# Attention's hand-written queues in a new order, in a three-stage decoder layer

## The chip, the core and the metric

The kernel runs on one core of one Trainium2 chip. The metric is the device time of one launch, in microseconds (us). Five engines work side by side, each through its own queue in program order, and meet only at semaphores: TensorE (PE; its weight loads are listed as PEld), VectorE (DVE), ScalarE (ACT), GpSimd (POOL), and SyncE (SP), which here only issues DMAs. An engine whose next instruction waits on a semaphore does nothing else meanwhile, so the order in which a queue is written decides what can run beside what.

## The reference, cut to what matters

The layer has three stages: a gated delta-rule attention, a state-space block, and a mixture-of-experts feed-forward. Only the attention is touched. For each of 16 heads and 4 batches of 512 tokens it computes:

```
q, k, v  = silu(causal conv of width 4 (x @ wq, wk, wv))          # 128 channels a head
gates    = small MLP of (entropy, |v - k@proxy|/|v|, cos, log1p|..|)   # 5 numbers a token
for rate in (slow, fast):                                          # two recurrences
    S_t  = S_{t-1} * decay_t + beta_t * k_t (v_t - k_t^T (S_{t-1} * decay_t))^T
    o_t  = q_t^T S_t
o        = lam * o_fast + (1 - lam) * o_slow
out      = o / rms(o) * onorm * sigmoid(gate)                      # then @ wo
```

## The kernel before, in words

Everything is float32, and a float32 matmul appears in the trace as two passes, so that every matmul of the program gives two weight loads and two MATMUL records.

**Units.** Head and batch make 64 units. A unit's 512 tokens are four chunks of 128, and there are two rates, so eight pairs of rate and chunk. `over_units` walks the slots: slots -3 to 5 are written out, then a loop of 13 turns (`TURNS`) runs four slots each, then the rest is written out. In slot `s` each engine's `slot(s)` works on several units at once, each at another stage of its life: `s.has(3)` and `s.has(2)` are units whose q, k and v are being projected, `s.has(1)` the unit whose gates and decay rows are made, `s.has(0)` the unit whose chunk matrices are built and inverted, `s.has(-1)` the one whose recurrence runs, `s.has(-2)` and `s.has(-3)` those whose output is normed and gated. `late` is the slot before. So each engine has one list of some 30 to 50 steps, which repeats once a unit, and `late` only says where the list is cut. The order in these lists is written by hand or by a planner outside; nothing in the kernel computes it.

**Steps on PE.** `project(i, k)` is one of four 128x512 matmuls that make k, v or q of a unit (L503). `products(level)` multiplies decayed keys with decayed keys and queries, in 32-wide blocks for levels 0 to 4 (L525: 32 small matmuls, 64 passes; I call these, and the next two, *fine groups*), wider ones for level 5 (L531) and 6 (L535). `w_fine_sum` (L549) and `x_fine_sum` (L560), levels 1 to 4, are the two halves of one step of a block inversion, again 64 passes each; `w_32_sum`, `xy_32_sum`, `w_64_sum` and `y_64_sum` (L627 to L658) are its wide end. `recur_even`, `recur_u`, `recur_odd` with a chunk number 0 to 3 are the recurrence over chunks (L573 to L616). `turn_v`, `proxy_v`, `gram_kq`, `turn_feats`, `hidden_1`, `hidden_2`, `heads_out`, `turn_rows` (L697) belong to the gates, `mean_square` (L692) and `gate_logits` (L706) to the output.

**The chain of levels.** `decay_nq(level)` on DVE (L1175 twice, then L1183) scales queries and keys for the next level: it waits for `products(level)` and `products(level + 1)` waits for it. `keep(level)` (L1194) masks a product into `apt_fine`, `grow(level)` (L1203, L1207) extends the inverse, `seed_y` and `turn_x0` start it. `copy_w` on ACT moves what `w_fine_sum` gave to SBUF for `x_fine_sum`.

**The chain of rows.** `heads_out` on PE, `add_z` on DVE, `tanh_t` on ACT, `gates_vals` on POOL, `turn_rows` on PE, `copy_rows` on ACT (L936); then SP (L447 to L456) writes the rows to DRAM, reads back the amplitude rows, then the amplitude sums, then the key rows, then the query rows, each hold waiting for the transfer before. `exp_e1` and `exp_tot` on ACT exponentiate them, `prepare_nq(NEG_K)` and `prepare_nq(QUERY)` on DVE (L1306, L1310) multiply them in, and `products(0)` of that unit waits for the last of these.

Of the kernel before, what the change touches and what calls it, by code (L numbers as in the profile page):

```python
# [136 lines left out]
def attn_stage(nc, io):  # L137

    with ExitStack() as ctx:
# [284 lines left out]
        with nc.Block() as block:  # L424
# [64 lines left out]
            def _(pe):  # L489
# [239 lines left out]
                def slot(s):  # L729
                    late = s.at(-1)  # L730
                    if late.has(0):
                        w_fine_sum(late, 2)
                    if late.has(-1):
                        recur_odd(late, 1)
                    if late.has(0):
                        products(late, 4)
                    if late.has(0):
                        x_fine_sum(late, 2)
# [4 lines left out]
                    if late.has(2):  # L743
                        gram_kq(late)
                    if late.has(0):
                        w_fine_sum(late, 3)
                    if late.has(0):
                        products(late, 5)
                    if late.has(-1):
                        recur_u(late, 2)  # L750
                    if late.has(-2):
                        mean_square(late)
                    if late.has(0):
                        x_fine_sum(late, 3)
                    if late.has(3):
                        project(late, 3, P_K, 2)
                    if late.has(3):
                        project(late, 3, P_K, 3)
                    if late.has(0):
                        w_fine_sum(late, 4)  # L760
                    if late.has(3):
                        project(late, 3, P_V, 0)
                    if late.has(-1):
                        recur_odd(late, 2)
                    if late.has(0):
                        x_fine_sum(late, 4)
# [4 lines left out]
                    if late.has(0):  # L771
                        w_32_sum(late)
                    if late.has(2):
                        turn_feats(late)
                    if late.has(-1):
                        recur_even(late, 3)
                    if late.has(3):
                        project(late, 3, P_V, 2)
                    if late.has(0):
                        xy_32_sum(late)  # L780
# [4 lines left out]
                    if late.has(-1):  # L785
                        recur_u(late, 3)
                    if late.has(0):
                        w_64_sum(late)
                    if late.has(-1):
                        recur_odd(late, 3)  # L790
                    if s.has(2):
                        project(s, 2, P_Q, 1)
                    if s.has(1):
                        hidden_1(s)
                    if s.has(2):
                        project(s, 2, P_Q, 2)
                    if late.has(0):
                        y_64_sum(late)
                    if s.has(0):
                        products(s, 0)  # L800
                    if s.has(-1):
                        recur_even(s, 0)
                    if s.has(2):
                        project(s, 2, P_Q, 3)
                    if s.has(-1):
                        recur_u(s, 0)
                    if s.has(1):
                        hidden_2(s)
                    if s.has(0):
                        products(s, 1)  # L810
                    if s.has(-1):
                        recur_odd(s, 0)
                    if s.has(1):
                        heads_out(s)
                    if s.has(2):
                        turn_v(s)
                    if s.has(0):
                        products(s, 2)
                    if s.has(-1):
                        recur_even(s, 1)  # L820
                    if s.has(0):
                        w_fine_sum(s, 1)
                    if s.has(2):
                        proxy_v(s)
                    if s.has(-3):
                        gate_logits(s)
                    if s.has(0):
                        x_fine_sum(s, 1)
                    if s.has(0):
                        products(s, 3)  # L830
                    if s.has(-1):
                        recur_u(s, 1)
                    if s.has(3):
                        project(s, 3, P_K, 0)
                    if s.has(1):
                        turn_rows(s)
# [4 lines left out]
            def _(act):  # L841
# [178 lines left out]
                def exp_tot(s):  # L1020
                    act.wait_ge(sums_in, s.due(1, 16, 16))
# [18 lines left out]
                def slot(s):  # L1040
                    late = s.at(-1)
                    if late.has(-1):
                        copy_kt(late, 0)
                    if late.has(-1):
                        copy_u(late, 0)
                    if late.has(1):
                        hide_2(late)
                    if late.has(2):
                        silu(late, 2, P_V)
                    if late.has(2):  # L1050
                        tap(late, 2, P_Q)
                    if late.has(-1):
                        copy_o(late, 0)
                    if late.has(1):
                        tanh_t(late)
                    if late.has(2):
                        keep_v(late)
                    if late.has(-2):
                        square_o(late)
                    if late.has(2):  # L1060
                        silu(late, 2, P_Q)
                    if late.has(0):
                        copy_w(late, 1)
                    if late.has(2):
                        square_v(late)
                    if late.has(-3):
                        tanh_gate(late)
                    if late.has(-1):
                        copy_kt(late, 1)
                    if late.has(-1):  # L1070
                        copy_u(late, 1)
                    if late.has(1):
                        copy_rows(late)
                    if late.has(-1):
                        copy_o(late, 1)
                    if late.has(0):
                        copy_w(late, 2)
                    if late.has(2):
                        square_vh(late)
                    if late.has(-1):  # L1080
                        copy_kt(late, 2)
                    if late.has(2):
                        square_err(late)
                    if late.has(0):
                        copy_w(late, 3)
                    if late.has(-1):
                        copy_u(late, 2)
                    if late.has(-2):
                        log_mean(late)
                    if late.has(3):  # L1090
                        tap(late, 3, P_K)
                    if late.has(0):
                        copy_32(late)
                    if late.has(2):
                        log_err(late)
                    if late.has(0):
                        copy_w(late, 4)
                    if late.has(-1):
                        copy_o(late, 2)
                    if late.has(1):  # L1100
                        exp_e1(late)
                    if late.has(1):
                        copy_ks(late)
                    if late.has(0):
                        copy_w(late, 5)
                    if late.has(0):
                        copy_64(late)
                    if late.has(2):
                        copy_feats(late)
                    if late.has(0):  # L1110
                        copy_xy32(late)
                    if late.has(3):
                        tap(late, 3, P_V)
                    if late.has(-1):
                        copy_u(late, 3)
# [4 lines left out]
                    if late.has(0):  # L1120
                        copy_w(late, 6)
                    if late.has(1):
                        exp_tot(late)
                    if s.has(1):
                        hide_1(s)
                    if late.has(-1):
                        copy_o(late, 3)
                    if late.has(3):
# [1365 lines left out]
```

## Time and profile before

| | us |
|---|---|
| median of 3 runs (lowest, highest) | 4910.75 (4907.41, 4925.25) |
| the profiled execution, and its span | 4893.68, 4891.9 |
| PE busy over the span | 4244.3 (87%) |
| DVE, ACT, POOL busy | 3329.3, 2248.5, 834.9 |

The attention fills the span from its start to about 3300 us; from 3400 us on the two other stages run. A busy PE is one with a matmul in flight. The idle time ahead of an instruction is put down to whatever released it; "issue" means that no semaphore explains it.

### The profile page before, as it was taken

The numbers are of one execution on the slowest core, as the hardware profiler recorded it, in microseconds if no ns is written. First come the engines' busy times: TensorE is split into PE (matmuls) and PEld (weight loads), VectorE is DVE, ScalarE is ACT, GpSimd is POOL, SyncE is SP. The second block draws the span as 40 slices with busy tenths as digits, with TensorE's granted clock in tenths as the row PEclk, the third lists the DMA queues.
The fourth block names the chain that finished last, engine by engine and source line by source line (L and its number), as shares of the span: only waits on it lengthen the run. The fifth ranks groups of instructions, "written<-read, shape, count | busy, mean of one in ns | idle before, by whom it ended". The sixth has DMA issues, their size and how long they took to land. (4 is left out here: it accounts for less than half of the span.)

```text
span 4891.9 us, 184831 instructions
## 1 busy us (share of the span) xinstructions
PE 4244.3 (87%) x76786; PEld 2657.1 (54%) x76786; DVE 3329.3 (68%) x5635; ACT 2248.5 (46%) x5484; POOL 834.9 (17%) x1800
## 2 busy tenths in 40 slices
PE   6789898988989888898988899975887786999999
PEld 4566666665666656666666666662333333444444
DVE  2678787777778777787777777864999995122121
ACT  2455565655556555555555555644344432111111
POOL 0222222322222222222222232220000000000000
PEclk9899999999999999999999999987898997999999
DMA  1111211112121111211111111112232334000000
GB/s 50 61 52 57 62 49 54 62 45 68 43 65 52 52 60 43 66 52 53 58 53 59 58 53 56 62 45 104 78 95 82 91 95 160 1 26 9 18 18 9
DMA packets 131630, 278.08 MB, mean 57 GB/s; under 512 B 20668, under 2 KB 62032, under 8 KB 127200
## 3 DMA queue, kind: packets, MB, share of 16 engines
q1 hardware_dynamic: 126176, 258.29, 16.8%
q8 instruction: 641, 10.50, 0.9%
q10 hardware_dynamic: 4608, 7.60, 0.4%
q14 instruction: 205, 1.68, 0.1%
HBM read 235.17 MB, written 30.67 MB: 54 GB/s over the span
## 5 line engine op out<-in xcount | busy, mean ns | idle before, releaser
L503 PE MATMUL a_pb<-a_x_t,a_w_qkv 128*128 128x512 f32 x1536 | 825.0, 634 | 24.4 <-DMA a_w_qkv<-in_w_qkv 12.2
L1175 DVE TENSOR_TENSOR a_nq<-a_nq,a_tot 128x512 f32<-128x512 f32 x768 | 516.8, 714 | 157.4 <-PE a_pb L535 62.1
L1151 DVE SCALAR_TENSOR_TENSOR a_acc<-a_pb,a_taps,a_acc 128x511 f32<-128x511 f32 (+2 forms) x576 | 429.7, 746 | 67.0 <-ACT a_acc L846 35.3
L1773 PE MATMUL m_p_y<-m_h,m_ident 128*128 128x512 f32 x512 | 292.2, 686 | 143.3 <-DVE m_h L1973 143.3
L525 PE MATMUL a_pb<-a_nq,a_ks 128*32 128x32 f32 x20480 | 250.6, 201 | 145.1 <-DVE a_ks L1183 126.6
L503 PEld LDWEIGHTS a_pb<-a_x_t,a_w_qkv 128*128 128x128 f32 x1536 | 250.4, 195 | 131.2 <-issue 104.6
L525 PEld LDWEIGHTS a_pb<-a_nq,a_ks 128*32 128x32 f32 x20480 | 218.6, 112 | 188.4 <-DVE a_nq L1175 135.2
L2241 PE MATMUL f_pb<-f_x_t,f_w_gu 128*128 128x512 f32 x704 | 308.0, 592 | 0.0
L549 PE MATMUL a_pb<-a_x_fine,a_apt_fine 32*32 32x16 f32 x16384 | 203.7, 183 | 107.3 <-issue 106.0
L1967 DVE TENSOR_TENSOR_SCAN m_h<-m_da,m_h 128x2048 f32<-128x2048 f32 x64 | 283.1, 4424 | 5.9
L549 PEld LDWEIGHTS a_pb<-a_x_fine,a_apt_fine 32*32 32x32 f32 x16384 | 173.5, 108 | 203.5 <-issue 189.8
L560 PEld LDWEIGHTS a_pb<-a_w_fine,a_y_fine 32*32 32x32 f32 x16384 | 176.9, 109 | 189.5 <-issue 178.9
L1183 DVE TENSOR_TENSOR a_ks<-a_ks,a_tot 128x512 f32<-128x512 f32 x384 | 274.5, 715 | 0.0
L2295 ACT ACTIVATE f_gate<-f_pb 128x512 f32<-128x512 f32 x132 | 78.8, 597 | 411.7 <-PE f_pb L2241 275.4
L1773 PEld LDWEIGHTS m_p_y<-m_h,m_ident 128*128 128x128 f32 x512 | 107.5, 220 | 293.4 <-DVE m_h L1973 170.2
L560 PE MATMUL a_pb<-a_w_fine,a_y_fine 32*32 32x16 f32 x16384 | 207.7, 183 | 66.1 <-issue 61.4
L1737 PE MATMUL m_p_o<-m_w_o,m_o_t 128*128 128x512 f32 x512 | 256.9, 622 | 0.0
L1194 DVE COPY_PREDICATED a_apt_fine<-a_mask_u,a_pb 128x256 f32<-128x256 int32 x320 | 179.4, 561 | 106.5 <-PE a_pb L549 106.4
L1896 ACT ACTIVATE m_da<-m_delta,m_neg_a 128x511 f32<-128x511 f32 x256 | 166.7, 711 | 182.5 <-DVE m_h L1967 180.1
L885 ACT COPY a_u_sb<-a_pb 128x256 f32<-128x256 f32 x256 | 95.4, 373 | 296.0 <-PE a_pb L593 296.0
L2241 PEld LDWEIGHTS f_pb<-f_x_t,f_w_gu 128*128 128x128 f32 x704 | 133.4, 190 | 166.4 <-issue 166.4
L2373 DVE TENSOR_TENSOR f_h_base<-f_gate,f_pb 128x512 f32<-128x512 f32 x44 | 30.2, 686 | 277.6 <-ACT f_gate L2295 277.6
(278 smaller groups left out, 8927.3 us busy)
## 6 DMA issues: line engine op xcount, KB each, us to landing
a_rows<-rows SPq DMA_DIRECT2D x192, 512.0 KB, 3.9
a_amp_sums<-amp_sums SPq DMA_DIRECT2D x64, 508.0 KB, 3.6
attn_o<-a_o_t SPq DMA_DIRECT2D x64, 256.0 KB, 2.6
m_b_rows<-ssm_bc SPq DMA_DIRECT2D x64, 256.0 KB, 3.7
m_c_rows<-ssm_bc SPq DMA_DIRECT2D x64, 256.0 KB, 4.6
m_o_t<-attn_o SPq DMA_DIRECT2D x14, 1024.0 KB, 8.6
a_w_qkv<-in_w_qkv SPq DMA_DIRECT2D x51, 256.0 KB, 2.8
f_w_gu<-in_w_gu SPq DMA_DIRECT2D x3, 1536.0 KB, 17.3
```

The lines of the kernel that those rows point to most:

```text
L503: mm = nc.tensor.matmul(pb[:, V_BANK if i == P_V else KQ_BANK], w_qkv[:, i, k], x_t[:, k, b * T:(b + 1) * T], start=(k == 0), stop=(k == D ...
L525: mm = nc.tensor.matmul(out.rearrange("p k (s h) -> p k s h", h=hs), ks[:, n2, rate, at], right(nq[:, n2, rate, :, at], hs), start=True, s ...
L549: mm = nc.tensor.matmul(w_psum[q, i].rearrange("p (s h) -> p s h", h=hs), apt_fine[q, i, NEG_K], left(x_fine[q, i:i + 1], hs)[:, 0], start ...
L560: mm = nc.tensor.matmul(x_psum[q, i], y_fine[q, i], w_fine[q, i], start=True, stop=True, tile_position=(g * BW, g * BW))
L1151: last = nc.vector.scalar_tensor_tensor(acc[:, i, d:T], src[:, 0:T - d], taps[:, i, 3 - d:4 - d], acc[:, i, d:T], ALU.mult, ALU.add)
L1175: last = nc.vector.tensor_tensor(part, part, spread(blocks, shape), ALU.mult)
L1183: nc.vector.tensor_tensor(part, part, spread(blocks.rearrange("p (s two) -> p s two", two=2)[:, :, 1:2], [P, T // hs, hs]), ALU.mult).then ...
L1194: nc.vector.copy_predicated(right(apt_fine[:].rearrange("p i k t -> p (i k) t"), hs), spread(compact(mask_u[:, level:level + 1], hs), [P, ...
L1737: mm = nc.tensor.matmul(p_o[:], o_t[:, q % 2, head], w_o[:, head], start=(head == 0), stop=(head == H - 1), skip_group_check=True)
L1773: nc.tensor.matmul(p_y[:, et], ident[:], h[:, (b * DS + n) % 3, et], start=(n == 0), stop=(n == DS - 1), skip_group_check=True).then_inc(s ...
L1967: nc.vector.tensor_tensor_scan(steps, da[:, row % 2].rearrange("p e t -> p (e t)"), steps, 0.0, ALU.mult, ALU.add).then_inc(scanned, 1)
L2241: mm = nc.tensor.matmul(out, w_gu[:, side, k, cols], x2_t[:, b % 2, k], start=(k == 0), stop=(k == DC - 1), skip_group_check=True)
```

## The change

The four lists are written in a new order; no matmul, vector or activation step is added or removed. Along with it come the edits that the new order needs:

```diff
 # PE: slot(), the list read round from its new start
+ x_fine 1, proxy_v, gate_logits, products 3, recur_u 1, turn_rows,
+ w_fine 2, recur_odd 1, mean_square, products 4, K 0, recur_even 2, K 1,
+ x_fine 2, recur_u 2, products 5, recur_odd 2, w_fine 3, gram_kq, K 2, recur_even 3, K 3,
+ x_fine 3, V 0, recur_u 3, w_fine 4, products 6, V 1, x_fine 4, V 2, recur_odd 3, w_32, V 3, Q 0,
+ xy_32, Q 1, products 0, w_64, Q 2, recur_even 0, turn_feats, y_64, products 1, Q 3, hidden_1,
+ recur_u 0, w_fine 1, hidden_2, recur_odd 0, products 2, heads_out, turn_v, recur_even 1
- w_fine 2, recur_odd 1, products 4, x_fine 2, recur_even 2, K 1, gram_kq, w_fine 3, products 5,
- recur_u 2, mean_square, x_fine 3, K 2, K 3, w_fine 4, V 0, recur_odd 2, x_fine 4, products 6, V 1,
- w_32, turn_feats, recur_even 3, V 2, xy_32, V 3, Q 0, recur_u 3, w_64, recur_odd 3, Q 1, hidden_1,
- Q 2, y_64, products 0, recur_even 0, Q 3, recur_u 0, hidden_2, products 1, recur_odd 0, heads_out,
- turn_v, products 2, recur_even 1, w_fine 1, proxy_v, gate_logits, x_fine 1, products 3, recur_u 1,
- K 0, turn_rows
 # DVE: slot()
+ seed_y, turn_x0, keep 1, decay 1, conv Q, new_state 0, add_z, decay 2, residual 1, grow 1, keep 2,
+ decay 3, dot_vvh, err_v, keep 3, new_state 1, decay 4, residual 2, gate_o, grow 2, decay 5,
+ new_state 2, keep 4, residual 3, gram_dots, grow 3, set_diag, conv K, prepare K, grow 4, decay 6,
+ prepare Q, invert, conv V, decay 0, keep 0
- decay 0, seed_y, keep 0, turn_x0, decay 1, new_state 0, keep 1, add_z, conv Q, residual 1, decay 2,
- dot_vvh, grow 1, keep 2, err_v, decay 3, keep 3, new_state 1, decay 4, grow 2, residual 2,
- gram_dots, keep 4, decay 5, grow 3, gate_o, invert, conv K, new_state 2, grow 4, decay 6,
- residual 3, prepare K, conv V, prepare Q, set_diag
```

(K, V, Q with a number is `project`; `decay` is `decay_nq`.) The ACT list is reordered likewise; its end now reads `copy_w 3`, `square_err`, `tap K`, `exp_tot`, `exp_e1`, `copy_w 4`, `copy_u 3`, `copy_ks`, `copy_64`, `scale_r0`, `root_rows`, `copy_w 5`, `tap V`, `copy_xy32`, `log_err`, `copy_w 6`, `silu K`, `copy_feats`, `copy_y64`, `copy_o 3`, `tap Q`, `hide_1`. Before, `log_err` stood a few steps behind `log_mean`, ahead of `exp_e1`, `root_rows` and `exp_tot`, and `tap Q` of a unit stood in the next slot, behind `silu V`. The single steps that change:

```diff
                 def exp_e1(s):
-                    if s.batch(1) == 0:
-                        head_col(decay, s, 1, C_DECAY)
...
                 def exp_tot(s):
+                    if s.batch(1) == 0:
+                        head_col(decay, s, 1, C_DECAY)
...
                     if level == 0:
                         need(dve, w_sum, s.due(-1, 6, 4))
-                    elif level > 1:
+                    elif level == 1:
+                        dve.wait_ge(product, s.due(0, LEVELS, 2))
+                    else:
                         dve.wait_ge(w_sum, s.due(0, 6, level - 1))
...
                 def gates_vals(s):
+                    pool.drain()
...
                 def norms_dens(s):
+                    pool.drain()
...
                 def slot(s):
-                    make_feats(s), spread_y(s), reset_y(s), spread_apt(s), gates_vals(s.at(1)), norms_dens(s.at(1))
+                    gates_vals(late), spread_apt(late), norms_dens(late), spread_y(late), make_feats(late), reset_y(late)
```

## Rows read from the trace of the kernel before

**Rows 1.** Windows: us, then busy time and instructions of each engine, clock, DMA share, GB/s.

```profile
600.00:3200.00 2600.00, 2306.50 (x59932) 1638.91 (x59933) 2014.06 (x4003) 1469.10 (x3958) 677.39 (x1459) 0.96 0.18 56
```

**Rows 2.** Groups by line, PE, 600 to 3200: busy, mean ns, idle before.

```profile
L503 PE MATMUL a_pb<-a_x_t,a_w_qkv 128*128 128x512 f32 x1246 | 667.4, 630 | 10.0 <-issue 9.6
L706 PE MATMUL a_pb<-a_g_t,a_g 128*128 128x512 f32 x104 | 59.1, 652 | 0.0
```

**Rows 3.** Waits of PE, 600 to 3200: total, times, longest.

```profile
PE a_pb L525 <- DVE a_ks L1183: 105.6, 144, 1.4
PE a_pb L549 <- issue: 85.4, 50, 3.8
PE a_pb L560 <- issue: 47.3, 45, 2.3
PE a_pb L593 <- issue: 17.2, 13, 1.5
```

**Rows 4.** Timeline of PE: start, length, line, matmul passes, idle before.

```profile
2008.88 1.05 PE L549 MATMUL a_pb<-a_x_fine,a_apt_fine 32*32 32x16 f32 x64 [3.51 <-issue]
...
2057.77 0.30 PE L549 MATMUL a_pb<-a_x_fine,a_apt_fine 32*32 32x16 f32 x11 [0.22 <-issue]
...
2059.53 0.76 PE L525 MATMUL a_pb<-a_nq,a_ks 128*32 128x32 f32 x64
2060.24 0.49 PE L560 MATMUL a_pb<-a_w_fine,a_y_fine 32*32 32x16 f32 x37
2062.46 0.51 PE L560 MATMUL a_pb<-a_w_fine,a_y_fine 32*32 32x16 f32 x27 [1.73 <-issue]
```

**Rows 5.** Windows between two breaks of PE, columns as in Rows 1.

```profile
2057.60:2062.00 4.40, 2.96 (x124) 2.68 (x125) 3.66 (x8) 1.57 (x10) 0.00 (x0) 1.00 0.04 7
2110.00:2115.00 5.00, 3.29 (x126) 2.32 (x126) 3.62 (x9) 1.88 (x11) 0.47 (x2) 1.00 0.53 97
2164.20:2168.50 4.30, 3.80 (x124) 2.73 (x124) 3.23 (x7) 1.61 (x3) 2.28 (x3) 1.00 0.48 138
```

**Rows 6.** DMA queues, 600 to 3200: packets, MB, share of 16 engines.

```profile
q8 instruction: 504, 8.26, 1.4%
```

**Rows 7.** A window across the loop's edge, columns as in Rows 1.

```profile
2008.00:2015.00 7.00, 6.12 (x206) 5.79 (x207) 2.17 (x5) 1.57 (x10) 0.00 (x0) 0.51 0.40 80
```

**Rows 8.** Timeline of DVE around one key decay.

```profile
2046.36 1.29 DVE L1175 TENSOR_TENSOR a_nq<-a_nq,a_tot 128x512 f32<-128x512 f32 x2 [0.16 <-issue]
2047.57 0.68 DVE L1183 TENSOR_TENSOR a_ks<-a_ks,a_tot 128x512 f32<-128x512 f32 x1
```

**Rows 9.** Timeline of PE: the product after a decay, then other steps.

```profile
2054.20 0.75 PE L525 MATMUL a_pb<-a_nq,a_ks 128*32 128x32 f32 x64 [0.81 <-DVE a_ks L1183]
...
2056.38 0.61 PE L697 MATMUL a_pb<-a_sum_w,a_vals 128*24 128x255 f32 x2
...
2091.71 0.77 PE L525 MATMUL a_pb<-a_nq,a_ks 128*32 128x32 f32 x64
```

**Rows 10.** Timeline of SP: the row transfers of one unit.

```profile
2057.99 0.32 SPq L447 DMA_DIRECT2D rows<-a_rows_sb  x1
...
2063.11 0.34 SPq L456 DMA_DIRECT2D a_rows<-rows  x1
2067.62 0.34 SPq L463 DMA_DIRECT2D a_amp_sums<-amp_sums  x1
2071.82 4.20 SPq L456 DMA_DIRECT2D a_rows<-rows  x2
```

**Rows 11.** The tile a_rows, 600 to 3200: us from issue to landing.

```profile
DMA to landing us min/median/max: 3.2/3.9/5.3
```

**Rows 12.** Groups by line, DVE then ACT, 600 to 3200.

```profile
L1306 DVE TENSOR_TENSOR a_nq<-a_kq,a_rows 128x1024 f32<-128x1024 f32 x104 | 127.0, 1221 | 11.2 <-PE a_pb L609 10.8
...
L995 ACT ACT_TABLE_LOAD x52 | 66.7, 1283 | 0.9
L1018 ACT ACT_TABLE_LOAD x52 | 66.7, 1283 | 3.0 <-DMA a_rows<-rows 1.1 <-issue 1.1
```

More of the change, by code:

```diff
@@ L731, in slot @@
                     if late.has(0):
+                        x_fine_sum(late, 1)
+                    if late.has(2):
+                        proxy_v(late)
+                    if late.has(-3):
+                        gate_logits(late)
+                    if late.has(0):
+                        products(late, 3)
+                    if late.has(-1):
+                        recur_u(late, 1)
+                    if late.has(1):
+                        turn_rows(late)
+                    if late.has(0):
                         w_fine_sum(late, 2)
@@ L742, in slot @@
                         project(late, 3, P_K, 1)
-                    if late.has(2):
-                        gram_kq(late)
                     if late.has(0):
-                        w_fine_sum(late, 3)
+                        x_fine_sum(late, 2)
+                    if late.has(-1):
+                        recur_u(late, 2)
                     if late.has(0):
@@ L771, in slot @@
                     if late.has(0):
[L772 to L776, printed above, removed]
+                        x_fine_sum(late, 4)
                     if late.has(3):
                         project(late, 3, P_V, 2)
+                    if late.has(-1):
+                        recur_odd(late, 3)
                     if late.has(0):
-                        xy_32_sum(late)
+                        w_32_sum(late)
                     if late.has(3):
@@ L1324, in slot @@
                     if late.has(0):
+                        keep(late, 1)
+                    if late.has(0):
                         decay_nq(late, 1)
-                    if late.has(-1):
-                        new_state(late, 0)
-                    if late.has(0):
-                        keep(late, 1)
-                    if late.has(1):
-                        add_z(late)
                     if late.has(2):
@@ L1334, in slot @@
                     if late.has(-1):
-                        residual(late, 1)
+                        new_state(late, 0)
+                    if late.has(1):
+                        add_z(late)
                     if late.has(0):
                         decay_nq(late, 2)
-                    if late.has(2):
-                        dot_vvh(late)
+                    if late.has(-1):
+                        residual(late, 1)
                     if late.has(0):
@@ L1353, in slot @@
                         decay_nq(late, 4)
+                    if late.has(-1):
+                        residual(late, 2)
+                    if late.has(-3):
+                        gate_o(late)
                     if late.has(0):
                         grow(late, 2)
+                    if late.has(0):
+                        decay_nq(late, 5)
                     if late.has(-1):
-                        residual(late, 2)
+                        new_state(late, 2)
+                    if late.has(0):
+                        keep(late, 4)
+                    if late.has(-1):
+                        residual(late, 3)
                     if late.has(2):
```

236 lines of the change are left out of this document (109 added, 127 removed).

## The prediction, on record before the changed kernel ran

> **What bounds the kernel now.** I read the windows first, to find which stretch counts and how full each engine is in it. From 600 to 3200 us the attention loop is steady: PE is busy for 2306.5 of 2600 us, DVE for 2014.1, ACT for 1469.1, POOL for 677.4 [rows 1]. One unit issues `gate_logits` once, in two passes; 104 records of it make 52 units [rows 2], so a unit takes 2600/52 = 50.0 us, and PE idles in it for 293.5/52 = 5.6 us. PE is the bound: the question is what its idle and slow time is made of.
>
> The waits of PE say it. 105.6 us are waits for DVE's key decay, that is 2.0 us a unit. The other 188 us, 3.6 us a unit, are nearly all "issue": no semaphore explains them, and they fall on the two fine inversion groups above all (85.4 and 47.3 us) [rows 3]. The timeline shows their form: a group breaks in its middle. At 2060.24 `x_fine_sum` runs 37 passes, PE stands for 1.73 us, then the other 27 follow; the break before was at 2057.77 [rows 4]. Between one such break and the next PE takes 124 to 126 matmuls and as many loads, three times over in different units [rows 5]; with the handful of semaphore instructions between them that is about 256 instructions, and the instruction queue moves 8.26 MB in 504 packets, 16 KB each [rows 6], which is 256 instructions of 64 bytes (my division; 504 packets for 52 units fit it too). So I read these breaks as PE running out of instructions at the end of a 16 KB piece. From resuming to resuming such a piece took 2062.46 - 2057.77 = 4.7 us, in windows of the same kind 4.3 and 5.0 [rows 4, 5], while two adjacent fine groups, 256 instructions, need 2 x 0.71 = 1.4 us (start to start, 2059.53 to 2060.24) [rows 4]. Once every four units, at the loop's edge, the break is 3.5 us before the slot's first group [rows 4].
>
> The Trainium skill ("Runtime: NRT & Kernel Launch", Instruction fetch mechanics) says that the queue is refilled in 16 KiB blocks and that crossing a block costs "one DMA tail-bump, mostly hidden". The block size agrees with the rows above; the word hidden does not, since 1.73 us stand open at one crossing. It speaks against the change: what it would make of the sum is rival A.
>
> Last the clock. Its mean is 0.96 [rows 1], the two levels are 1.2 and 2.4 GHz, so 8% of the time, 4.0 us a unit, is at the lower one and costs about half of that, 2.0 us. The low stretches follow the breaks: after the one at the loop's edge seven microseconds stand at 0.51 [rows 7], and groups of 0.7 us take 1.05.
>
> So 50.0 = 42.4 of matmuls at the high clock + 2.0 waits for decays + 3.6 breaks (0.9 of them the loop's edge, 3.5/4) + 2.0 low clock (some 0.8 of it the edge).
>
> **The change, part by part.** Work stays the same: nothing is removed, so the 42.4 stay.
>
> *Long steps between fine groups.* Before, `x_fine 1` and `products 3` stand back to back, so do `products 4` and `x_fine 2`, and `w_fine 3`, `products 5`, `gram_kq` form another thick place; 800 instructions further on there are stretches with four projections and hardly an instruction. After, each fine group has at least a projection, a recurrence step or the output matmul behind it. I walked both lists with the lengths of the rows (fine group 0.7, a projection 2 x 0.48, a recurrence step 0.5 to 1.4, and so on) and took at every possible place the time of the next 256 instructions. Before, the shortest stretch is 1.4 us and 54% of the places lie under 3.9 us; after, 2.3 us and 29%. With 9.2 pieces a unit (1152 matmuls and loads each a unit, 125 of each a piece [rows 1, 5]) the shortfall under 3.4 us adds to 1.6 us a unit before and 0.6 after, under 3.9 us to 4.0 and 1.5. The measured 3.6 - 0.9 = 2.7 lies between the two, and the new list gives by the same reading about 1.0. Waits and low clock, which stretched pieces before, shrink, so I take 1.2. Bounds: 0.5, and, if a piece needs 4.4 us everywhere, 3.4. The loop's edge stays as it is, 0.9: the break comes from the jump back, and the first group behind it is now `x_fine 1` in place of `w_fine 2`.
>
> *Decays in front.* A decay takes DVE 1.29 + 0.68 us less an overlap, so 1.9 us from its start to the last key [rows 8]; with the hop a product can start 2.1 us after the one before it ended. Before, less than that lay between `products 1`, `2` and `3` on PE, and each waited, 0.81 us at 2054.20 [rows 9]. After, PE has 3.8 us between `products 0` and `1` (`w_64`, `Q 2`, `recur_even 0`, `turn_feats`, `y_64`), 3.7 between 1 and 2, and 4.2 between 2 and 3 (cyclically), and on DVE `decay 0` runs before `seed_y` and the new unit's copies, `decay 2` right behind `add_z`. But `conv Q` (2.4 us) now stands before `new_state 0` and `decay 2`. Working DVE's list against PE's, `decay 2` ends 1.3 us before `products 3` is due. The 2.0 us go to 0.3; bounds 0 and 1.5.
>
> *The chain of rows, new and tight.* From `turn_rows` to the end of the last row transfer the trace has 2056.38 to 2071.82 + 4.2 + 3.9 = 2079.9, thus 23.5 us, made of an ACT copy and four transfers in a row [rows 9 to 11]. Before, `products 0` came at 2091.71, 35.3 us after `turn_rows` [rows 9], and this was covered by 11.8 us. After, `turn_rows` stands some 7 steps earlier relative to `w_fine 2` but the long steps it had behind it are spread, and PE's own work from `turn_rows` to `products 0` is 26.8 us. DVE must fit in behind the transfers: key rows land at about 19.6, `prepare K` 2.5 (1.22 and 1.27), `grow 4` 0.8, `decay 6` 2.0, `prepare Q` 2.5 = 27.4 us, and ACT's `square_o` stands before the copy of the rows, +0.2. So `products 0` is 0.8 us late in each unit: a new wait, `products 0` on DVE's L1310, with `w_64`, `Q 2` and all else queued behind it. It is bounded by 0 (PE's breaks in these 26.8 us hide it) and by 4 x (5.3 - 3.9) = 5.6 us more if every transfer takes the longest time of the rows [rows 11]; I take 0.8.
>
> *DVE.* Its list, start to start, adds to 39.6 us a unit (seven decays 13.8, three convolutions 7.1, two preparations 5.1, the rest 13.6), near PE's 42.4, so it can absorb little. It has no wait in my walk but 1.4 us before `keep 1` and 1.2 before `residual 3`. `gram_dots` moves behind `residual 3`, and `V 0`, which waits for it, is due just then: 0 to 0.5, inside the terms above.
>
> *ACT.* `log_err` now comes after the exponentials: ln, exp, ln, silu in place of ln, exp, silu. Both kinds had a load of their own, 52 times 1.283 us [rows 12], so one more load a unit on an engine that is busy for 28.3 of 50 us. It falls between `copy_xy32` and `copy_w 6`, where `Q 1`, `products 0` and `w_64` run on PE for 2.8 us and ACT needs 2.6. Cost 0, at most 0.5 if that cover is gone. The skill ("ScalarE: Activation LUTs", Table sets: the hidden batching unit) has exp and ln in one set, and by it the move would cost no load at all; the trace loads for each, so I go by the trace.
>
> *POOL* gets two drains a unit, a few tenths of a us of an engine that is busy for 13.0 of 50; its longest new chain, norms 5.6 us, then `spread_y` 3.8, ends 0.6 us before `w_64` needs it. Cost 0, at most 0.5.
>
> *Clock.* The edge's share stays at 0.8; the rest, 1.2, follows the breaks and falls to 0.5. Bounds 0.2 and 1.2.
>
> **Sum for a unit:** 42.4 + 0.3 + 0.9 + 1.2 + 0.8 + 0.8 + 0.5 = 46.9 us, or 3.1 less than 50.0. Of 64 units about 60 run with full queues: -186 us. Against the profiled execution's own 4893.7 us that is 4708; the median of the runs lies 17 us above it, so 4725 is what I predict.
>
> **The rivals.**
> *A, the breaks stay (0.20).* If PE's breaks come from something that the order does not touch, as the skill's rule would have it, only the decays' 1.7 us go and the rows' 0.8 come: 0.9 x 60 = 54 us, 4857. Against it: the breaks' equal distance in instructions [rows 5]. For it: the pieces took 4.3 to 5.0 us where they broke, and if each needs 4.4 the new list still falls short by 3.4 us.
> *B, the rows' chain decides (0.10, slower).* One mechanism: the four transfers in a row, now 0.8 us longer, with what DVE does behind them, than PE covers. A unit is then the chain, 27.6, plus PE from `products 0` to `turn_rows`, 15.1, plus the edge and breaks in that part, 3.0: 45.7, which is hidden in the sum. Each us by which the transfers lengthen adds one; from +4.3 us on the kernel is slower than before. At 5.3 us a transfer it is +5.6: 51.3 a unit, 4990. For it: instruction pieces and rows now share the queues more closely; against: the median is 3.9 [rows 11].
> *C, DVE becomes the bound (0.20).* With 39.6 us of its own plus 1.4 + 1.2 of waits and what PE's breaks pass on, it holds the unit at 48.3: -1.7 x 60 = -102, 4810.
> *D, it does nothing measurable (0.05),* gains and new waits cancel: 4911.
> The forecast itself has 0.45.
>
> **How the numbers follow.** 0.5% is about what a measurement of this kernel can tell from no change, 25 us. Forecast, A and C are faster: 0.85; D is same, 0.05; B is slower, 0.10. The forecast's own range, with the bounds of the breaks (0.5) and the waits (0), is 44.9 to 48 a unit, 4605 to 4790. For eight times in ten I leave out B, D and the lowest corner: 4630 to 4865.
>
> **What would show it.** PE's waits for L1183 under 30 us in all; "issue" at L549 and L560 together halved, with what is left at the loop's edge; a new wait of `products 0` for L1310 of some 0.8 us a unit; the clock at 0.97 to 0.98; DVE busy over 80% of the stage; 64 more table loads. It is wrong if the breaks keep their sum, or if a wait of L525 for L1310 grows over 3 us a unit.

## The result, and the profile after

The changed kernel takes 4641.8 us in the median of 4 runs (4634.4 to 4649.3), the kernel before 4909.1 in 4 runs beside them. The ratio is 0.945, 95% interval 0.942 to 0.948: 267 us less. 4725 was forecast, with 4630 to 4865 as the range, so direction and range held, and the gain was 1.4 times what the sum gave.

The slices of PE on the page of before, then the totals and the slices on the page of after:

```profile
PE   6789898988989888898988899975887786999999
```

```profile
PE 4218.0 (91%) x76786; PEld 2643.4 (57%) x76786; DVE 3308.5 (71%) x5635; ACT 2295.2 (49%) x5544; POOL 965.2 (21%) x1800
...
PE   6899999999999999999999999867778787999999
```

The same 76786 matmul passes, the same 5635 DVE instructions, and 60 more of ACT, all of them table loads (64 were forecast); PE's busy time hardly moved (4244.3 before). What went is idle time. The window over the attention loop, columns as in Rows 1, and the count of units in it:

```profile
600.00:3000.00 2400.00, 2281.64 (x60138) 1629.93 (x60137) 1994.34 (x3998) 1513.15 (x3997) 789.38 (x1460) 0.97 0.20 61
```

```profile
L706 PE MATMUL a_pb<-a_g_t,a_g 128*128 128x512 f32 x104 | 61.0, 672 | 0.0
```

Again 104 passes, 52 units, now in 2400 us instead of 2600 [rows 1, 2]: 46.15 us a unit, 3.85 less than before, and 64 x 3.85 = 246 of the 252 us between the two profiled executions (4893.7 and 4642.0). PE idles for (2400 - 2281.6)/52 = 2.3 us a unit in place of 5.6. Its waits, which answer to [rows 3]:

```profile
PE a_pb L560 <- issue: 31.4, 20, 3.4
PE a_pb L605 <- ACT a_u_sb L885: 23.5, 11, 2.5
PE a_pb L525 <- DVE a_nq L1312: 13.7, 24, 2.7
PE a_pb L650 <- POOL a_y_inv L1478: 11.3, 51, 0.3
PE a_pb L549 <- issue: 9.5, 22, 0.9
...
PE a_pb L525 <- DVE a_ks L1183: 2.4, 12, 0.2
```

Three things stand out, each over 52 units. The wait for key decays (L1183) fell from 105.6 us to 2.4. "Issue" over all lines fell from 180 us to 50, and what is left of it is mostly the loop's edge, the place where each engine jumps back to the start of its loop: 12 times some 2.5 us at L560. And there are waits that were not there: for ACT's `copy_u` 11 times, for `prepare Q` (L1312), for POOL's `spread_y`. A unit as a sum, the clock's share estimated as in the prediction from the mean granted clock:

| us a unit | before | forecast | after |
|---|---|---|---|
| matmuls at the high clock | 42.4 | 42.4 | 42.5 |
| waits for key decays | 2.0 | 0.3 | 0.05 |
| "issue": edge and breaks | 3.6 | 2.1 | 1.0 |
| wait for L1312 | 0 | 0.8 | 0.3 |
| other waits | under 0.1 | 0 | 0.9 |
| low clock (mean 0.96, 0.97) | 2.0 | 1.3 | 1.4 |
| sum | 50.0 | 46.9 | 46.15 |

The first and the sixth row are an estimate, and e3 below allows a check of it: there PE ran at clock 1.00 and was busy for 43.0 us a unit. By that the matmuls are half a microsecond more than in the first row, and the low clock as much less.

### The profile page after: what moved, and what is told of

It is laid out like the page before. It is cut to its first block and busy times, and to the rows that moved or that the text cites. A ratio compares the mean times of both kernels' runs of the same rounds, so it can differ in the third digit from the quotient of the medians.

```text
span 4639.8 us, 185070 instructions
## 1 busy us (share of the span) xinstructions
PE 4218.0 (91%) x76786; PEld 2643.4 (57%) x76786; DVE 3308.5 (71%) x5635; ACT 2295.2 (49%) x5544; POOL 965.2 (21%) x1800
## 5 line engine op out<-in xcount | busy, mean ns | idle before, releaser
L503 PE MATMUL a_pb<-a_x_t,a_w_qkv 128*128 128x512 f32 x1536 | 835.8, 636 | 12.9 <-DMA a_w_qkv<-in_w_qkv 12.3
L525 PEld LDWEIGHTS a_pb<-a_nq,a_ks 128*32 128x32 f32 x20480 | 218.6, 113 | 206.4 <-issue 113.0
L1463 POOL COPY a_apt<-a_apt_fine 32x256 f32<-32x256 f32 x256 | 100.5, 393 | 969.1 <-DVE a_apt_fine L1196 943.6
L503 PEld LDWEIGHTS a_pb<-a_x_t,a_w_qkv 128*128 128x128 f32 x1536 | 238.8, 190 | 96.2 <-issue 59.1
L525 PE MATMUL a_pb<-a_nq,a_ks 128*32 128x32 f32 x20480 | 255.8, 202 | 38.3 <-DVE a_nq L1312 29.1
L1183 DVE TENSOR_TENSOR a_ks<-a_ks,a_tot 128x512 f32<-128x512 f32 x384 | 275.0, 716 | 0.0
L560 PEld LDWEIGHTS a_pb<-a_w_fine,a_y_fine 32*32 32x32 f32 x16384 | 166.2, 106 | 185.8 <-issue 178.1
L885 ACT COPY a_u_sb<-a_pb 128x256 f32<-128x256 f32 x256 | 95.0, 371 | 327.5 <-PE a_pb L593 285.6
L846 ACT ACTIVATE a_acc<-a_pb,a_taps 128x512 f32<-128x512 f32 x192 | 131.9, 687 | 214.8 <-PE a_pb L503 214.8
L1478 POOL COPY a_y_inv<-a_y_fine 32x256 f32<-32x256 f32 x256 | 221.3, 864 | 32.8
L560 PE MATMUL a_pb<-a_w_fine,a_y_fine 32*32 32x16 f32 x16384 | 192.8, 181 | 35.1 <-issue 34.3
```

The lines of the kernel that those rows point to most:

```text
L503: mm = nc.tensor.matmul(pb[:, V_BANK if i == P_V else KQ_BANK], w_qkv[:, i, k], x_t[:, k, b * T:(b + 1) * T], start=(k == 0), stop=(k == D ...
L525: mm = nc.tensor.matmul(out.rearrange("p k (s h) -> p k s h", h=hs), ks[:, n2, rate, at], right(nq[:, n2, rate, :, at], hs), start=True, s ...
L560: mm = nc.tensor.matmul(x_psum[q, i], y_fine[q, i], w_fine[q, i], start=True, stop=True, tile_position=(g * BW, g * BW))
L1183: nc.vector.tensor_tensor(part, part, spread(blocks.rearrange("p (s two) -> p s two", two=2)[:, :, 1:2], [P, T // hs, hs]), ALU.mult).then ...
L1478: last = nc.gpsimd.tensor_copy(y_inv[q, s.ring(0, 2), :, q], y_fine[q])
```

## The experiments

All times are medians; the ratio to the kernel before, run on the same chip, is given with its interval. Windows are 600 to 3000 us.

**e6: are the breaks ends of 16 KB pieces?** 128 semaphore increments on PE's queue ahead of the first slot.

```diff
+                for _ in range(128): pe.sem_inc(passed, 1)
                 over_units(pe, slot)
```

> The kernel before, with 128 semaphore increments on PE's queue ahead of its first slot, so that everything behind them lies half a 16 KB piece later in the instruction stream. Theory (a break stands where a piece of 256 instructions ends): all breaks keep their distance of 256 but their place in the stream moves by 128 instructions against the steps; those of before at 178 or 179 after the loop's edge (modulo 256) stand at about 50. The time may move by up to 1% either way, since other steps are hit. Rival (a break belongs to a step, or to what the step waits for): same steps, same passes as before.

4949 us, ratio 1.010 (1.006 to 1.014). I counted every record of PE from one jump back to the next. In the kernel before, all of the breaks in the middle of work stand at 185 or 186, modulo 256, after the jump; here all of them stand at 59 or 60: 126 earlier in the turn, the same in every turn looked at. The waits for L1183, which belong to steps, kept their places but for two records (such as the 2235th, now the 2237th), so that against the steps the breaks moved by 128, as many as were put in. The waits show the lines that were hit before no longer hit [rows 3 has L593 and L503], and others in their place:

```profile
PE a_pb L525 <- DVE a_ks L1183: 99.4, 121, 1.3
PE a_pb L549 <- issue: 90.8, 54, 3.0
PE a_pb L560 <- issue: 43.4, 42, 2.0
PE a_pb L531 <- issue: 22.6, 11, 2.8
PE a_pb L525 <- issue: 20.8, 17, 1.7
PE a_pb L578 <- issue: 11.4, 12, 1.3
```

So a break belongs to the 256th instruction, not to a step. That is shown. The time moved too: "issue" grew from 3.6 us a unit to 4.1 and the clock sank from 0.96 to 0.95, which together make the 1%.

How long must 256 instructions take for no break to come? I took all pieces in the trace of before from the first jump back, at 593 us, to 3150 us, and called a stand of over 0.15 us at their end a break. Of the pieces whose work takes less than 3.5 us 75 end in a break and 44 do not; of those from 3.5 to 5 us 32 do and 134 do not. From resuming to resuming a broken piece takes 4.2 us in the median, and nine in ten lie between 3.4 and 5.6. It is a matter of odds and not a sharp bound.

**e1: long matmuls between fine groups, and nothing else.**

```diff
 # PE list of the kernel before
+ ..., products 4, K 1, x_fine 2, ..., w_fine 3, K 2, products 5, ..., x_fine 3, K 3, w_fine 4, ...
+ ..., proxy_v, x_fine 1, gate_logits, products 3, ...
```

> The kernel before, with four PE steps moved so that a long matmul stands between neighbouring fine groups (gate_logits between x_fine 1 and products 3, K 1 between products 4 and x_fine 2, K 2 between w_fine 3 and products 5, K 3 between x_fine 3 and w_fine 4); DVE, ACT and POOL lists as before. Theory (a break comes when 256 instructions need less than 3.4 to 3.9 us): walked like the other lists, this one falls short by 1.6 to 3.7 us a unit against 1.6 to 4.0 before, so next to nothing is won: 4890 to 4910 us; the waits for the key decays stay at 2.0 us a unit. Rival (neighbouring fine groups themselves are the trouble): the breaks halve, 1.4 us a unit with their clock share, 4820.

4896.6 us, ratio 0.995 (0.993 to 0.997): 24 us less, a tenth of the gain, and inside what was expected. The window holds 48 units:

```profile
PE a_pb L549 <- issue: 109.5, 67, 3.8
PE a_pb L525 <- DVE a_ks L1183: 63.1, 92, 1.2
PE a_pb L560 <- ACT a_w_fine L867: 27.6, 38, 0.8
PE a_pb L560 <- issue: 14.1, 24, 1.0
PE a_pb L593 <- issue: 13.6, 11, 1.6
```

Together with its smaller rows "issue" is 160 us, 3.3 a unit against 3.6 before in the same window. Putting one long step between two neighbours moves instructions by a few places; how long 256 of them take is decided over several steps. The rival, that neighbours are the trouble, falls: it wanted the breaks halved. One thing came otherwise than expected: the wait for key decays was to stay at 2.0 us a unit and fell to 1.3, because `x_fine 1` came sooner and now waits for ACT's `copy_w 1` itself, 0.6 us a unit (L867), and `products 3` behind it no longer waits.

**e5 and e2: neighbours again, in the changed kernel.** e5 moves two steps and nothing late comes of it; e2 makes three pairs (its first stands in the order `gate_logits`, `proxy_v`, `x_fine 1`, `products 3`).

```diff
 # e5
- x_fine 1, proxy_v, gate_logits, products 3
+ proxy_v, gate_logits, x_fine 1, products 3
```

```diff
 # e2, further
- products 4, K 0, recur_even 2, K 1, x_fine 2, recur_u 2, products 5, recur_odd 2, w_fine 3
+ K 0, recur_even 2, K 1, products 4, x_fine 2, recur_u 2, recur_odd 2, products 5, w_fine 3
```

> The changed kernel, with one pair of fine groups back to back: proxy_v and gate_logits stand ahead of x_fine 1 instead of between it and products 3. No other step moves. Theory (breaks by count of instructions): the shortfall rises by 0.5 us a unit at either bound (0.6 to 1.1, 1.5 to 2.1), with its clock share 0.8 x 64 = 51: 4690. Rival (all that the run with three pairs lost is due to the pairs, 100 us each): 4740. Second rival (it was all due to steps that came late there, none by breaks): 4642.

> The changed kernel, with fine groups put back to back in three places on PE (x_fine 1 and products 3; products 4 and x_fine 2; products 5 and w_fine 3), the long steps standing ahead of the pairs; all other lists as changed. Theory: the shortfall rises by 1.0 us a unit (0.6 to 1.5 under 3.4 us, 1.5 to 2.7 under 3.9), plus its share of low clock: 4642 + 64 x 1.2 = 4720, with more breaks inside L549, L560 and L525. Rival (the gain came from the waits and the chain of levels, breaks do not matter): within 15 us of 4642.

e5: 4671 us, ratio 0.953 (0.950 to 0.957), 30 us more than the changed kernel by the medians and 41 by the two ratios, where 48 were expected. Its "issue" in the middle of work grew, L549 from 9.5 to 25.3 and L525 from 2.5 to 13.0, and over all lines from 1.0 us a unit to 1.4:

```profile
PE a_pb L549 <- issue: 25.3, 39, 1.1
...
PE a_pb L525 <- issue: 13.0, 16, 1.2
```

e2: 4941 us, ratio 1.005 (1.003 to 1.007). The whole gain is gone and 300 us were lost where 78 were expected. The trace says why that is not the price of neighbours:

```profile
PE a_pb L593 <- DVE a_r_sb L1256: 56.2, 37, 1.8
PE a_pb L605 <- ACT a_u_sb L885: 45.3, 59, 2.4
PE a_pb L560 <- issue: 35.0, 26, 2.5
PE a_pb L706 <- issue: 31.4, 11, 3.8
PE a_pb L549 <- issue: 28.9, 37, 1.4
```

`products 4` behind K 1 makes `decay 4` late on DVE, `residual 2` stands behind it in DVE's list, and `recur_u 2` and `recur_odd 2` wait for that. Of 4.9 us a unit (47 units in the window) the new waits for L1256 and L885 are 1.7, "issue" 1.4, and the clock, 0.94 in place of 0.97, about 1.6. As a test of neighbours e2 was confounded by my moving a step of the chain of levels; e5 is the clean one, for one of the three pairs.

**e9: the decay in front of the seeds.**

```diff
 # DVE list; keep 0 also waits for products 0 itself
- conv V, decay 0, keep 0, [next slot] seed_y, turn_x0, keep 1
+ conv V, keep 0, [next slot] seed_y, turn_x0, decay 0, keep 1
```

> The changed kernel, with decay 0 behind keep 0, seed_y and turn_x0 on DVE instead of ahead of them (keep 0 waits for products 0 itself). Theory (in the trace of after, decay 0 ends 0.2 us before products 1 starts, and the three steps take 1.2 us): products 1 is 1.0 us late in each unit, 4642 + 64 = 4706, and PE's waits at L525 for L1183 grow to some 50 us in the loop. Rival (the later steps on PE take it up): 4642 to 4655.

4800 us, ratio 0.978 (0.974 to 0.982): 158 us more than the changed kernel, where 64 were expected. The wait is the one that was named:

```profile
PE a_pb L525 <- DVE a_ks L1183: 96.7, 50, 4.6
```

In the unit looked at amid the loop it is one wait of 1.22 us. In the trace of after the decay ends at 2061.16 + 0.69 and `products 1` starts at once:

```profile
2061.16 0.69 DVE L1183 TENSOR_TENSOR a_ks<-a_ks,a_e 128x512 f32<-128x512 f32 x1
```

```profile
2062.09 0.77 PE L525 MATMUL a_pb<-a_nq,a_ks 128*32 128x32 f32 x64
```

The rest is the longest wait, 4.6 us, once a turn: the place where DVE's list is cut now lies ahead of `decay 0`. DVE's own jump back (2.6 us before `seed_y`, 11 times, in this run's trace) falls into the chain, and the clock sinks to 0.95 behind it. The 1.2 us are shown as the value of this order; how the remaining 80 us divide between edge and clock is argued from the rows. The kernel before also had `decay 0` ahead of the seeds, so e9 prices a good place that the change kept, and no part of the 267 us.

**e3 and e10: the loop written out.**

```diff
-    for n in range(-3, FIRST_TURN):
-        slot(Slot(n))
-    with engine.Fori(0, TURNS) as turn:
-        for j in range(B):
-            slot(Slot(FIRST_TURN + j, turn))
-    for n in range(FIRST_TURN + B * TURNS, UNITS + 4):
+    for n in range(-3, UNITS + 4):
         slot(Slot(n))
```

> The changed kernel without the loop: all 71 slots written out. Theory (the jump back costs PE 2.5 us and ACT 3.5 us of stand, of which 2.1 us reach PE as a wait for copy_u 0, and some 5 us at the low clock behind them): 13 turns x (2.5 + 2.1 + 2.5) = 92 us less, 4550. Rival (the breaks at the loop's edge are those of the 16 KB pieces and come anyway): 4620 to 4640.

> The kernel before without the loop, all slots written out. Theory (the edge costs 3.4 us of stand and as much at the low clock behind it, ACT's own edge is hidden in this order): 13 x 6.8 = 88 us less, 4820. So the new order, both written out, would be worth 4820 - 4537 = 283 us and does not live off the edge. Rival (the old order's breaks take back what the edge frees): 4870.

e3: 4537 us, ratio 0.923 (0.921 to 0.925), the fastest of all and 105 us less than the changed kernel. e10: 4807 us, ratio 0.979 (0.975 to 0.983), 102 less than before. So the edge costs about 100 us in either order, 8 us a turn, and the new order is worth 270 us without it, as much as with it. Each order came close to its expectation (4550 and 4820).

In e3 the attention ends inside the window (its last `gate_logits` is at 2970.9 us), so its steady part is read from 600 to 2600:

```profile
600.00:2600.00 2000.00, 1951.86 (x52364) 1389.55 (x52362) 1743.21 (x3497) 1328.70 (x3506) 690.09 (x1280) 1.00 0.21 63
```

At 1152.5 passes a unit that is 44.0 us a unit against 46.0 in after counted the same way, of which PE idles for 1.1 (2.3 in after) and is busy for 43.0 (43.7). The granted clock is 1.00: without the edge no low stretch is left in the new order, though some breaks are. In e10 the clock is 0.97 in the same window. PE's waits in e3, 600 to 3000, are down to these, others of the attention of 6 us and less, and one wait behind its end:

```profile
PE a_pb L525 <- DVE a_nq L1312: 13.9, 24, 2.9
PE a_pb L650 <- POOL a_y_inv L1478: 12.7, 50, 1.6
PE a_pb L549 <- issue: 9.0, 16, 1.5
PE a_pb L525 <- issue: 6.9, 11, 1.6
```

**e4: ACT's list cut elsewhere.** The first ten ACT steps stand at the end of the slot before; their order is the same.

```diff
-                    if late.has(-1):
-                        copy_u(late, 0)
...
+                    if s.has(-1):
+                        copy_u(s, 0)
```

> The changed kernel, with ACT's list cut at another place: its first ten steps (copy_u 0 to copy_kt 1) stand at the end of the slot before, so that ACT's jump back falls ahead of square_v, where ACT waits for PE anyway; the order of its steps is the same. Theory: PE's wait at L605 for L885, 2.1 us a turn, goes, with some clock: 13 x 2.1 to 13 x 3 = 27 to 40 us less, 4605 to 4615. Rival (that wait is hidden behind DVE or the rows): 4642.

4633 us, ratio 0.943 (0.941 to 0.945), which cannot be told from the changed kernel's 0.945 (0.942 to 0.948); 4605 to 4615 was expected. The wait of L605 for L885 is gone from the rows, as the theory said, but "issue" at L560 rose from 31.4 to 39.9 and at L525 from 2.5 to 17.2:

```profile
PE a_pb L560 <- issue: 39.9, 25, 3.4
PE a_pb L525 <- issue: 17.2, 19, 1.4
```

All "issue" together went from 50 us to 78, so the 23.5 us of the wait came back whole in the window. That PE reaches its next piece sooner and stands there instead fits this, and was not tested further.

**e7, e11, e12: has the chain of rows any slack?** `turn_rows` behind `recur_odd 1` (e7); in addition `mean_square` behind K 0 (e11); written out, with `turn_rows` ahead of `recur_u 1` (e12).

```diff
 # e7
- recur_u 1, turn_rows, w_fine 2, recur_odd 1, mean_square, products 4, K 0
+ recur_u 1, w_fine 2, recur_odd 1, turn_rows, mean_square, products 4, K 0
 # e11
+ recur_u 1, w_fine 2, recur_odd 1, turn_rows, products 4, K 0, mean_square
 # e12 (with e3's edit)
+ turn_rows, recur_u 1, w_fine 2, recur_odd 1, mean_square, products 4, K 0
```

> The changed kernel, with turn_rows behind recur_odd 1 instead of ahead of w_fine 2, so that the rows' chain starts 2.1 us later and products 0 of the unit is where it was. Theory (the chain from turn_rows to products 0 has no slack left; the trace of after has PE waiting 0.3 us a unit for it): at least 1.5 us a unit, 4642 + 64 x 1.5 to 2.1 = 4740 to 4775, with the wait of L525 for L1312 grown to some 90 us in the loop. Rival (there is slack of 2 us or more, PE's wait comes from elsewhere): below 4665.

> As the run with turn_rows behind recur_odd 1, but with mean_square moved behind K 0 too, since there it waited 0.6 us a unit for the rows' copy and hid what the chain does. Theory (the rows' chain has about 1 us of slack against products 0): of the 2.1 us by which it starts late 1.1 show, PE's wait at L525 for L1312 grows from 14 to some 50 us or more in the loop, 4642 + 64 x 1.1 = 4712. Rival (slack of more than 2 us; the 108 us of that run were mean_square's wait and breaks alone): within 20 us of 4642.

> The changed kernel without the loop, with turn_rows one step earlier, ahead of recur_u 1, so that the rows' chain starts 0.5 us sooner. Theory (what is left of PE's wait for L1312, 13.9 us in 56 units, goes): 0.25 x 64 = 16 us less than the 4537 of the unrolled kernel, 4521. Rival (turn_rows then waits for POOL's gates, and recur_u 1 behind it comes late): 4550 to 4570.

e7: 4750 us, ratio 0.967 (0.963 to 0.971), inside what was expected, but not for the reason given: the wait for L1312 stayed at 16.4 us, and `mean_square` waited for the rows' copy 50 times. e11 was to take that away: 4738 us, ratio 0.966 (0.963 to 0.969), and a third wait came in its place:

```profile
PE a_pb L503 <- ACT a_gate L952: 39.5, 51, 1.1
PE a_pb L560 <- issue: 37.2, 21, 3.8
PE a_pb L605 <- ACT a_u_sb L885: 22.3, 11, 2.3
...
PE a_pb L525 <- DVE a_nq L1312: 16.0, 29, 0.8
```

K 0 waits for `tanh_gate`, which stands behind `copy_rows` in ACT's list. e12 started the chain 0.5 us sooner and changed nothing: 4539 us, ratio 0.926 (0.923 to 0.929), against e3's 0.923 (0.921 to 0.925), with 16.3 us of waits for L1312 against 13.9.

So starting the chain 2.1 us late costs about 100 us, and starting it early wins nothing. The 100 us have more than one part. The new wait behind ACT's copy is 0.6 us a unit in e7 and 0.8 in e11 (50 units); "issue" rose by 0.7 in both, to 84 us; and DVE waits for the rows' transfers more often than in after, where it is 11 times:

```profile
DVE a_nq L1308 <- DMA a_rows<-rows: 28.1, 22, 2.4
```

(e7; in e11 28 times.) So the transfers had little slack left at their place.

**e8: `log_err` back ahead of the exponentials.**

```diff
 # ACT list
- square_err, tap K, exp_tot, exp_e1, copy_w 4, ..., copy_xy32, log_err, copy_w 6
+ square_err, tap K, log_err, exp_tot, exp_e1, copy_w 4, ..., copy_xy32, copy_w 6
```

> The changed kernel, with log_err ahead of exp_tot on ACT, where it stood before the change relative to the exponentials, so that a unit needs three table loads and not four. Theory (the fourth load is hidden behind Q 1, products 0 and w_64): within 10 us of 4642. Rival (it delays copy_w 6 and so y_64, 0.3 us a unit): 4620.

4885 us, ratio 0.996 (0.994 to 0.998): neither was near. The table loads went from four kinds to three, as said. But `log_err` waits for POOL's norms, and these for `gram_dots`, and that stands late in the new DVE list:

```profile
ACT a_feats L991 <- POOLq L1443: 198.0, 49, 4.1
```

```profile
PE a_pb L560 <- ACT a_w_fine L867: 141.5, 48, 3.3
```

ACT stands for 4 us a unit with `copy_w 4` queued behind it, and PE for 3. One step at the wrong place of an in-order list undoes the whole change. The price of the fourth load by itself was therefore not measured; in after no PE wait names `copy_w 6` (L873) or `copy_y64`, which fits a price of nothing but does not show it.

## Why the prediction was right, and where its sizes were off

- **"1.0 ... I take 1.2" for breaks at piece ends, 0.9 for the edge.** The mechanism is shown by e6. The walk over 256 instructions is borne out by e1 (0.3 us a unit less "issue" expected at most, 0.2 to 0.3 found) and e5 (0.5 more expected, 0.5 found). This is the term that was most mis-sized: all "issue" in after is 1.0 us a unit, some 0.6 of it the edge, so 0.4 remained of the 1.2. The walk itself had given about 1.0 and even 0.6 at its lower bound; I had added to it because waits would no longer stretch the pieces. PE's edge shrank as well, from about 3.5 us to 2.5, without my having seen why.
- **"The 2.0 us go to 0.3."** They went to 0.05, for the reason given. I took the time from the end of each key decay to the first weight load of the products that wait for it, in 42 units amid the run (the 11th to the 52nd). For `products 1`, `2`, `3`, `4` the medians are 0.12, 0.12, 0.12 and 1.01 us before, so that the first three start on the heels of the decay, and 0.24, 1.0, 1.4 and 2.3 after. The 1.4 in front of `products 3` had been forecast as 1.3. One reading was wrong: between `products 2` and `3` of before PE had 5.0 us, 0.8 of them waiting, and not "less than that". `decay 2` was late there because DVE ran `conv Q` and `residual 1` first; it starts 3.0 us behind the end of `products 2`:

```profile
2049.10 2.38 DVE L1151 SCALAR_TENSOR_TENSOR a_acc<-a_pb,a_taps,a_acc 128x511 f32<-128x511 f32 x3
2051.40 0.59 DVE L1254 SCALAR_TENSOR_TENSOR a_r_sb<-a_v_tok,a_beta_v,a_pb 128x128 f32<-128x128 f32 x2
2052.16 1.29 DVE L1175 TENSOR_TENSOR a_nq<-a_nq,a_tot 128x512 f32<-128x512 f32 x2 [0.16 <-issue]
```

  In after `conv Q` starts 1.0 us before `products 2`, `residual 1` stands behind `decay 2`, and `decay 2` starts 1.2 us behind the end of `products 2`:

```profile
2065.84 2.39 DVE L1151 SCALAR_TENSOR_TENSOR a_acc<-a_pb,a_taps,a_acc 128x511 f32<-128x511 f32 x3
...
2068.81 1.29 DVE L1175 TENSOR_TENSOR a_nq<-a_nq,a_tot 128x512 f32<-128x512 f32 x2 [0.16 <-issue]
```

  No run puts these steps alone back to their old places; the share of the decays rests on the two traces. Nor was `decay 0` moved ahead of `seed_y` by the change, as the prediction has it: it stood there before.
- **"`products 0` is 0.8 us late": the rows' chain.** The wait is there in every unit, but smaller. In all of the 42 units the first weight load of `products 0` starts 0.05 us behind the end of `prepare Q`, and from `turn_rows` to `products 0` it is 27.7 us in the median, where 27.6 was forecast. The 0.8 was mis-sized because PE's own way there, with its breaks, is nearer 27.4 than 26.8: PE stands idle for 0.3 us a unit, and where the wait is shorter the matmul before is still running. Which part of the chain decides was seen only in part. Going back from the end of `prepare Q`, DVE works without a pause for 13.5 us, from `residual 3`, which waits for `recur_even 3` on PE, in 33 of the 42 units; in 7 the pause is for the rows' transfers. So it is mostly DVE's list from `residual 3` on, `conv K` within it, that holds `products 0`, and e12 fits that: starting the rows earlier won nothing. The prediction also counts four transfers in a row, where rows 10 show five issues one behind the other (a write and four reads), of which three are of the tile whose longest is 5.3 us; this changes only the bound of 5.6.
- **Rival B (slower) and C.** B fell: the transfers did not lengthen, in after the last two are issued 13.8 us behind the first (2088.93 and 2075.14), as before [rows 10]. C, DVE as the bound, fell as to the time: 4642 and not 4810, DVE busy for 83% of the stage and PE for 95%. Its mechanism is at work in one stretch, the one ahead of `products 0`.
- **Rival A, the rule that a crossing is hidden.** It would have left 3.6 us of breaks in place; they went to 1.0, and e6 shows them at crossings. The Trainium skill ("Runtime: NRT & Kernel Launch", Instruction fetch mechanics) has the cost as "mostly hidden" and blocks of 16 KiB. Here the measurement decides against it as to the cost, and agrees as to the size of a piece.
- **ACT and POOL at nothing.** Not quite: ACT's own loop edge came to stand in PE's way (23.5 us, 0.45 a unit, e4), and POOL's `spread_y` by 0.2 us in every unit. These and smaller ones, 0.9 us of other waits, were in no term. Breaks, edge and the two waits for DVE came out 1.8 us a unit lower than forecast, and the other waits took back half of it.
- **"About 60" units.** 64 fits the measured time; that is 15 us of the difference between 186 and 252.
- **Clock.** 1.3 forecast, 1.4 found by the same estimate, mean 0.97. The sum is right and the parts are not: 0.8 was for the edge and 0.5 for breaks, and in e3 the clock is 1.00 although some breaks are left, so that in the new order all of the low clock went with the edge, PE's and ACT's. In the old order it did not: e10 has 0.97. That the sum agrees is luck.
- **The range.** Its lower end, 44.9 us a unit, is 45.1 with the bounds that the prediction names for it. Nothing hangs on the difference.

## What to carry to other kernels

Where small matmuls run by the hundred, count instructions and not only their time: in this kernel's trace PE mostly stood where 256 of them needed less than about 3.5 us, and less and less often above that; a list can be checked for that with a running sum before anything is built. 128 idle instructions ahead of the loop moved the whole kernel by 1% (e6), so two orders that differ by that little may differ only in where their pieces end. Judge a moved step by what is queued behind it on its own engine (e2, e8, e11: 100 to 300 us each), and mind where each engine's list is cut, for each has its own jump back. Writing the loop out took 2% off both orders.

## What the runs showed of the hardware that was not expected

The same POOL instruction with the same operands takes longer in the new order, though nothing in it changed: `a_dens` from 368 to 1128 ns in the mean, the copies of `spread_y` from 647 to 871, while `spread_apt` fell from 539 to 393.

```profile
L1478 POOL COPY a_y_inv<-a_y_fine 32x256 f32<-32x256 f32 x208 | 181.1, 871 | 26.6
...
L1463 POOL COPY a_apt<-a_apt_fine 32x256 f32<-32x256 f32 x212 | 83.2, 393 | 801.3 <-DVE a_apt_fine L1196 780.0 <-issue 1.3
...
L1447 POOL TENSOR_TENSOR a_dens<-a_norms 128x4 f32<-128x4 f32 x52 | 58.7, 1128 | 3.3
```

The means hide three distinct lengths, and which one comes depends on what DVE runs beside it. In after, over the whole run, a copy of `spread_y` takes 0.40 us beside `conv V` (61 copies), 0.67 beside the last part of a decay (64), and 1.21 beside either half of `prepare Q` (126). `a_dens` takes 0.20 us beside nothing and 1.19 beside the second half of `prepare` (54 of 64 times). The POOL instruction thus lasts about as long as the one of DVE beside it, 0.7 us for 512 columns of a decay and 1.2 for the 1024 of `prepare`. In the kernel before `spread_y` already ran beside `decay 6`; new is `prepare Q` beside it. It was felt on DVE too: `decay 6` takes 1.49 + 0.88 us there, and 1.29 + 0.68 elsewhere. That the one makes the other wait is what these rows show by where they coincide; no run moves one of the two alone, and the profile's spans on POOL are rough.
